# Moving the last sums and products of an attention-and-experts kernel between VectorE's steps, and one sum to GpSimd

## The reference

```python
xn = _layernorm(x)
s = attention(xn, Wq, Wk, Wv, Wo)      # 16 query heads, 4 key heads, rotary, causal softmax
g = _silu(experts(xn))                 # 16 routed experts, 2 per token, plus a shared one
x = x + s * g
```

## Time and profile before

| | us |
|---|---|
| median of 3 runs | 671.11 |
| range of the runs | 670.66 to 671.42 |
| the profiled execution's own time | 674.29 |
| its span in the trace | 672.4 |

### The profile page before, as it was taken

One profiled execution on the slowest core, in us unless ns is written; L12 is line 12 of the kernel. 1 busy time (PEld: TensorE's weight loads), 2 busy tenths in 40 slices (PEclk: granted clock), 3 DMA queues, 4 the chain that ended last, 5 costly groups with the idle time before them and its releaser, 6 DMA issues.

```text
span 672.4 us, 15653 instructions
## 1 busy us (share of the span) xinstructions
PE 644.5 (96%) x5124; PEld 462.9 (69%) x5187; DVE 543.5 (81%) x1644; ACT 458.2 (68%) x1221; POOL 475.0 (71%) x545
## 2 busy tenths in 40 slices
PE   8888999999999999999999999999999999999994
PEld 6655767767677676767776776767776777776772
DVE  6999999999999999999999999999974553333356
ACT  5587877877686766767676766768697845555542
POOL 4878777687667676687787878776769945555454
PEclk9999999999999999999999999999999999999998
DMA  9980001011600000000000101000144716665874
GB/s 298 347 245 2 1 1 33 9 25 25 170 1 1 1 1 1 1 26 34 26 32 16 40 8 40 16 26 1 41 67 142 201 28 138 139 142 136 231 262 148
DMA packets 70816, 52.11 MB, mean 77 GB/s; under 512 B 41376, under 2 KB 64128, under 8 KB 70752
## 3 DMA queue, kind: packets, MB, share of 16 engines
q1 hardware_dynamic: 66688, 40.83, 22.6%
q0 software_dynamic: 3792, 10.43, 4.9%
q10 hardware_dynamic: 272, 0.02, 0.0%
HBM read 24.75 MB, written 18.77 MB: 65 GB/s over the span
## 4 chain that ended last, share of the span: by engine, by line
PE 74%; DVE 12%; ACT 7%; issue 4%; POOL 1%; DMA 1%; DVEq 0%; ACTq 0%; POOLq 0%
PE bank L1622 12%; PE bank L1560 12%; PE bank L1639 10%; PE bank L1767 10%; PE bank L1591 10%; PE bank L1606 8%; PE bank L1801 7%; PE bank L1776 3%; DVE arena L1279 2%; PE bank L1575 2%; ACT arena L930 2%; DVE arena L1252 2%; DVE arena L1251 1%; ACT arena L944 1%; ACT arena L938 1%
## 5 line engine op out<-in xcount | busy, mean ns | idle before, releaser
L639 POOL TENSOR_TENSOR arena<-arena,rinv 128x64 f32<-128x64 f32 (+2 forms) x192 | 102.0, 559 | 74.0 <-DVE rinv L1273 74.0
L930 ACT ACTIVATE arena<-bank,nmax 128x448 f32<-128x448 f32 (+7 forms) x256 | 125.6, 506 | 40.3 <-DVE nmax L1267 39.9
L944 ACT CAST arena<-bank 128x512 f16<-128x512 f32 (+1 forms) x192 | 94.4, 523 | 43.4 <-PE bank L1606 42.5
L1560 PE MATMUL bank<-xnT_both,arena 128*128 128x512 f16 (+2 forms) x435 | 114.5, 380 | 5.2 <-DVE arena L1252 1.2
L1622 PE MATMUL bank<-arena 128*128 128x512 f16 (+7 forms) x751 | 113.9, 298 | 2.2 <-DVE arena L1284 1.3
L1267 DVE CUSTOM_DVE_ANT_0 bank<-bank,mask_b 128x448 f32<-128x448 f32 (+7 forms) x256 | 109.4, 485 | 6.6 <-issue 6.5
L1279 DVE TENSOR_TENSOR arena<-bank,arena 128x512 bf16<-128x512 f32 (+1 forms) x192 | 108.7, 594 | 4.3 <-ACT arena L944 3.6
L627 POOL TENSOR_TENSOR arena<-arena 128x512 f32<-128x512 f32 x79 | 100.6, 1273 | 12.6 <-DVE s_sb L1295 8.5
L1591 PE MATMUL bank<-arena 128*128 128x448 bf16 (+3 forms) x767 | 104.7, 286 | 2.1 <-ACT arena L930 1.0
L632 POOL TENSOR_TENSOR arena<-arena 128x512 bf16<-128x512 f32 x80 | 92.3, 1163 | 16.1 <-ACT arena L918 15.9
L1606 PE MATMUL bank<-ident_f,arena 128*128 128x128 f32 x640 | 94.2, 275 | 5.1 <-DVE arena L1279 3.8
(11 more groups left out here) (162 smaller groups left out, 1096.9 us busy)
## 6 DMA issues: line engine op xcount, KB each, us to landing
stage<-w_gate_up SPq DMA_DIRECT2D x16, 352.0 KB
xs_dram<-compare SPq DMA_DIRECT2D x3, 1560.0 KB, 15.5
arena<-ys_dram SPq DMA_DIRECT2D x8, 512.0 KB, 7.9
stage<-w_down SPq DMA_DIRECT2D x16, 176.0 KB
stage<-wq SPq DMA_DIRECT2D x4, 512.0 KB, 9.3
stage<-wo SPq DMA_DIRECT2D x4, 512.0 KB, 9.8
stage<-x SPq DMA_DIRECT2D x1, 2048.0 KB
out<-s_sb SPq DMA_DIRECT2D x7, 256.0 KB, 2.1
```

Source lines behind the costliest of these rows:

```text
L639: ins = pool.tensor_tensor(pr, pr, rinv[:, par, qt:qt + 1].to_broadcast([P, n]), ALU.mult)
L930: ins = act.activation(probs[par][:, P_AT[qt]:P_AT[qt] + n], score_bank[u][:, col:col + n], ACT.Exp, scale=-1.0, bias=nmax[:, par, qt:qt + ...
L944: act.copy(pT[j % 2][0][:, at:at + cols], pt_bank[(3 * j + u) % 2][:, 0:cols]).then_inc(pt_hi, 1)
L1560: ins = pe.matmul(ps[:], w[a][:, c * chunk:c * chunk + DH], tokens[m][:, c * TOK:c * TOK + S], start=(c == 0 and n == 0), stop=(c == KC - ...
```

## The change

After the steps, sums 2, 3 and 4 no longer stand on VectorE: sum 2 comes after step 76 (behind product 0), and sums 3 and 4 after step 78. Product 2 comes after step 79 and product 3 after step 80; within one step products now come ahead of sums. Gate 2 moves from step 80 to step 78, gate 3 to step 79 and gate 4 to step 80. The sum of part 5 with x moves from VectorE (L1456, counted by `late_out`) to GpSimd (L870, counted by `summed`), and SyncE's waits follow.

```diff
-END_SUMS = {-5: 0, -4: 1, 0: 2, 1: 3}
-END_PRODUCTS = {-3: 0, -2: 1}
-END_GATES = {-4: 0, -3: 1, 1: 2}
+END_SUMS = {-5: [0], -4: [1], -3: [2], -1: [3, 4]}
+END_PRODUCTS = {-3: 0, -2: 1, 0: 2, 1: 3}
+END_GATES = {-4: 0, -3: 1, -1: 2, 0: 3, 1: 4}
...
             for g, t in enumerate(PARTS):
-                if g < EARLY_GROUPS:
+                if g <= EARLY_GROUPS:
                     sp.wait_ge(summed, g + 1)
                 else:
-                    sp.wait_ge(late_out, g - EARLY_GROUPS + 1)
+                    sp.wait_ge(late_out, g - EARLY_GROUPS)
...
             for g in range(EARLY_GROUPS):
                 add_pair(g)
-            for g in range(EARLY_GROUPS):
+            for g in range(EARLY_GROUPS + 1):
                 add_x(g)
...
             def end_parts(n):
-                if n in END_SUMS:
-                    add_shared(END_SUMS[n])
                 if n in END_PRODUCTS:
                     multiply(END_PRODUCTS[n])
+                for g in END_SUMS.get(n, []):
+                    add_shared(g)
...
             ffn_steps(step)
-            add_shared(EARLY_GROUPS - 1)
             for g in range(len(END_PRODUCTS), EARLY_GROUPS):
                 multiply(g)
             multiply(EARLY_GROUPS)
             multiply(EARLY_GROUPS + 1)
-            add_x(EARLY_GROUPS)
             add_x(EARLY_GROUPS + 1)
```

## The result

The changed kernel takes 672.31 us (median of 8 runs, 671.75 to 674.04), the kernel before, on the same chip, 671.01 us (median of 8, 670.48 to 671.42), so that the medians are 1.3 us apart. The ratio is 1.0021, with a 95% interval of 1.0012 to 1.0030, which makes 1.4 us: the interval excludes no difference, but the change is only at the edge of the 0.2% (1.3 us) that the prediction counts as none. The forecast was 671.2 us, its range 669.2 to 672.0.

A forecast was written before the change was run, and what follows sets the result against it. The prediction took the end to be bound by VectorE's queue, then GpSimd's, then the stores. The last store would be issued about 0.1 us later, so 671.11 + 0.1 = 671.2 us, range 669.2 to 672.0.

The forecast's parts named there:

- The turns of VectorE and GpSimd: Two-SBUF-input VectorE sums and GpSimd instructions exclude each other; sums 3 and 4 take 2.8 us instead of 1.2.
- The first rival: Milder blocking in the last steps: sums take 0.6 us each, TensorE bounds, 1.9 us less, 669.2 us; chance 0.22.
- the late low part: Low part of step 79 on VectorE, behind sum 4: 1.5 us late, giving back most of the chain's 1.8 us.
- The second rival: Sum 2 loses its turn to GpSimd's pair sum: 0.6 us more, 671.7 us; chance 0.11 together with late data.
- The upper case of the second rival: Sum 2 losing its turn, plus one more lost turn (1.25 us): 672.4 us.
- The slower rival: Sum 2 loses its turn; x of part 5 ends on GpSimd at 667.1, four stores queue behind: 671.7 us; chance 0.11 with late data.

The follow-up runs named there:

- e3: The changed kernel run once more, unaltered, beside the kernel before: ratio to before 1.0008 [0.9994, 1.0021], tail 24.5 us.
- f2: The kernel before plus a late one-column memset at the end of GpSimd's queue, waiting for VectorE's last sum: ratio 1.0045 to before.
- e2: The kernel before with only the sum of part 5 with x moved to GpSimd: ratio 1.0016 to before.
- e4: The kernel before run again unchanged: ratio 1.0008 [0.9997, 1.0018] to before, tail 23.3 us.
- h3: The changed kernel with only sum 4 moved, to after step 79: ratio 1.0003 to before.
- e1: The changed kernel with the sum of part 5 with x back on VectorE: ratio 0.9987 to before.
- f1: The kernel before with x of part 4 moved to VectorE, so that GpSimd ends with part 3: ratio 0.9973 to before.
- f3: The changed kernel with x of parts 4 and 5 on VectorE: ratio 0.9978 to before.
- f4: The kernel before with x of parts 3 and 4 moved to VectorE: ratio 0.9972 to before.
- h1: The changed kernel with sum 4 behind the low part of step 79 and x of parts 4 and 5 on VectorE behind product 5: ratio 0.9949 to before.
- h2: As h1, with sum 2 after step 78, sums 3 and 4 after steps 79 and 80, later products and gates: ratio 0.9950 to before.

## Why the prediction was wrong

The step that failed is in its first paragraph: "SyncE issues the last store at 667.96, and 4.4 us follow to the end of the span; the change doesn't touch them." The 4.4 us were taken as a fixed step behind the last store. Only 2.2 of them were (the store's landing). In the other 2.2 SyncE was done and the program waited for GpSimd, whose DRAIN runs to 6.55 us behind its last instruction. By the working's own number for that instruction, x of part 5 at 666.6 against 665.66 before, the sum would have been +0.9 us instead of +0.1: 672.0 us, 0.3 short of what was measured.

Point by point, in positions behind the anchor (the prediction's, less 649.15; the measured ones, less 645.90):

| step | predicted | measured |
|---|---|---|
| sum 2 starts, ends | 5.05, 5.95 | 5.15, 6.06 |
| hidden product of step 77 | 6.07 | 6.19 |
| sums 3 and 4 start, end | 7.9, 10.7 | 8.0, 10.6 |
| low part of step 79 | 10.65 | 10.56 |
| product 2 | 11.15 | 11.09 |
| product 6 ends | 14.8 | 14.8 |
| x of part 5 ends on GpSimd | 17.45 | 17.25 |
| VectorE ends | 18.65 | 18.39 |
| last store issued | 18.9 (18.65 to 19.05) | 18.75 |
| end of the span | 23.35 | 24.0 |

- The turns of VectorE and GpSimd were right in this trace, and within 0.3 us everywhere. The first rival (milder blocking, 669.2 us) is refuted by 2.65 us for sums 3 and 4.
- That the three sums leave VectorE's chain and most of the gain comes back as the late low part was right: product 2 is 0.4 us earlier, product 6 not at all.
- What bounds the end was wrong: not VectorE, then the stores, but GpSimd. The row with the 1.80 us sum ending at 665.66 was the one that set the time, and it was read only as the thing that VectorE's sums wait for.
- The second rival (sum 2 loses its turn) was given too small a chance. It doesn't appear in the first trace, but in e3 it costs 0.5 us of the tail, and in 4 of 5 later traces with that place of sum 2 it happened. It fits the spread of the changed kernel's runs (671.75 to 674.04, against 670.48 to 671.42 before), which no trace of the slower ones was taken to show.
- The upper case of the second rival doesn't add up as it stands: 671.7 + 1.25 is 672.95, not 672.4. A range that reached half-way to it would have ended at 672.3, which is what was measured, but by another mechanism: it would have been right by luck.
- The slower rival named the right instruction and the wrong zero: "the point where x of part 5 ends later than about 666.5; each 0.1 beyond is 0.1 at the end". By the closing rows each 0.1 us beyond 665.66 counted.

In the changed kernel's trace sum 3, behind GpSimd's x of part 0, and sum 4, behind x of part 1, took 0.97 and 1.75 us. By the rule of the Trainium skill, "SBUF — State Buffer", section "Who interferes with whom" (one of the two engines has the shared port for its whole instruction and the other blocks), the trace agrees, at these numbers: both ended 0.55 us behind GpSimd's sum. Who gets the turn is less regular than the prediction took it to be. In f2 VectorE did its three sums in a row, unhindered, while GpSimd's x of part 1, listed as begun ahead of them, took 3.14 us:

```profile
657.64 3.14 POOL L870 TENSOR_TENSOR s_sb<-s_sb,stage 128x512 f32<-128x512 f32 x1
```

```profile
657.76 1.88 DVE L1445 TENSOR_TENSOR row_sb<-row_sb,arena 128x512 f32<-128x512 f32 x3
```

What decides a turn was not tried.

## What to carry to other kernels

Before costing an edit near the end of a kernel, look at the closing rows of every engine: the last engine to be done is the one whose queue counts, and it may be one whose last instruction lies 7 us ahead of the end. Work that is moved off a busy engine onto the one that is done last is paid for in full there, while work moved the other way (x of part 4 from GpSimd to VectorE) gained 1.8 us though VectorE looked like the bound. And an early place in an in-order queue is only free if the data are there in every execution: sum 2 had 1.3 us to spare in the one trace it was planned from, and none in 9 of the 13.

## What the runs showed of the hardware

- GpSimd's closing DRAIN ended 6.55 us behind its last instruction in all thirteen traces, the same within 0.02 us behind a 0.10 us memset as behind a 1.73 us sum. Those of VectorE, ScalarE and TensorE ended within 0.1 us behind theirs (VectorE's 0.4 us in the list begins while its last sum still runs), and SyncE's took 0.01 us. Whether the 6.55 us depend on the indirect transfers that GpSimd issued earlier in this kernel was not tried.
- The last store's landing, from issue to the end of SyncE's wait, took 2.2 us in the traces of before, e2, e3, e4, f2, h3 and of the changed kernel and 1.7 to 1.8 us in e1, f1, f3, f4, h1 and h2. It did not differ between the traces of before and of the changed kernel.
- Where a VectorE sum of two SBUF inputs was held up by a GpSimd sum, it ended 0.55 us behind GpSimd's with 512 columns, in all 13 traces, and 0.28 us with 256, in four. With further sums ready on both engines they mostly alternated instruction by instruction; in f2 VectorE had three turns in a row.
- The TensorE clock granted to the whole span was 0.994 to 0.998 of full speed in all traces. In the tail it stayed at the full level until TensorE was through in twelve of them. In h1 it was half for 3.4 us, after TensorE had stood idle for 1.69 us, and the four matmuls of 512 columns took 2.90 us instead of 1.98.
